# One fused attention and feed-forward kernel: the pair of quads combined from the pv bank, jobs and extras placed anew

## The reference

```
q  = layernorm(x) @ Wq.T + bq, scaled by 1/4       16 heads of 16 columns
k  = ctx @ Wk.T + bk        v = ctx @ Wv.T + bv
a  = softmax(q k^T) v        for each head          512 x 512 scores
y  = x + a @ Wo.T + bo
h  = (layernorm(y) @ W1[b].T + b1[b]) @ W2[b].T + b2[b]
out = y + h
```

## Time and profile before

| | us |
|---|---|
| median of 3 runs | 575.1 |
| profiled execution | 571.25 |
| its span | 569.5 |
| TensorE busy (PE) | 529.5, 93% |
| DVE busy | 442.7, 78% |
| ACT busy | 383.8, 67% |
| GpSimd busy (POOL) | 277.4, 49% |

### The profile page before, as it was taken

The page is one execution under the profiler, slowest core; times in us unless marked ns, Lnnn a source line. Parts: engine busy times, 40 slices in busy tenths (PEclk is TensorE's granted clock), DMA queues, the critical chain, the costliest instruction groups (busy, mean ns, idle before and its releaser), DMA issues.

```text
span 569.5 us, 13271 instructions
## 1 busy us (share of the span) xinstructions
PE 529.5 (93%) x4229; PEld 334.3 (59%) x4229; DVE 442.7 (78%) x805; ACT 383.8 (67%) x707; POOL 277.4 (49%) x314
## 2 busy tenths in 40 slices
PE   8899999999999889997999979999799989899997
PEld 6564556665666565664666656566466656354556
DVE  4888886898788986899778997789968887776114
ACT  6347778777876658775676747767487777667732
POOL 3946434576247814566335743367234782107211
PEclk9989999999999989999999989999899999898999
DMA  6773064615355243523446133470425424340201
GB/s 205 203 242 95 3 150 114 231 33 135 101 156 174 59 131 76 224 74 75 111 113 232 28 94 93 114 258 2 120 70 141 157 59 131 79 168 0 88 9 37
DMA packets 34367, 65.29 MB, mean 115 GB/s; under 512 B 9810, under 2 KB 11930, under 8 KB 32282
## 3 DMA queue, kind: packets, MB, share of 16 engines
q1 hardware_dynamic: 34330, 64.81, 38.7%
HBM read 34.65 MB, written 4.44 MB: 69 GB/s over the span
## 4 chain that ended last, share of the span: by engine, by line
PE 67%; DVE 12%; POOL 9%; issue 6%; ACT 2%; DMA 1%; SPq 0%; DVEq 0%; POOLq 0%; ACTq 0%
PE pv L560 16%; PE st L546 13%; PE misc L673 9%; PE nat L529 8%; PE misc L645 7%; DVE neg_max L1037 7%; PE misc L632 7%; POOL b_part L1334 3%; POOL b_part L1329 3%; POOL y L1322 2%; DVE y L1103 2%; ACT probs L861 2%; DVE stats L1048 2%; PE misc L609 1%; PE nat L585 1%
## 5 line engine op out<-in xcount | busy, mean ns | idle before, releaser
L1037 DVE TENSOR_REDUCE neg_max<-nat 128x1 f32<-128x512 f32 x512 | 328.4, 679 | 64.1 <-PE nat L529 62.2
L861 ACT ACTIVATE probs<-st 128x512 f32<-128x512 f32 x505 | 289.9, 598 | 123.7 <-PE st L546 111.5
L529 PE MATMUL nat<-ks,qs 63*128 63x512 f32 x512 | 241.3, 495 | 13.0 <-DVE neg_max L1037 10.4
L546 PE MATMUL st<-qs,ks 64*128 64x512 f32 x505 | 233.2, 489 | 4.6 <-ACT probs L861 3.9
L546 PEld LDWEIGHTS st<-qs,ks 64*128 64x128 f32 x505 | 92.1, 189 | 78.6 <-ACT probs L861 54.4
L560 PE MATMUL pv<-probs,vs 128*32 128x512 f32 x1024 | 126.0, 610 | 0.0
L529 PEld LDWEIGHTS nat<-ks,qs 63*128 63x128 f32 x512 | 94.2, 188 | 29.4 <-DVE neg_max L1037 22.6
L673 PE MATMUL misc<-w_in 64*128 64x256 f32 x512 | 75.6, 387 | 0.0
L1305 POOL TENSOR_TENSOR attnT<-pair_ctx,inv_sum 128x512 f32<-128x512 f32 x15 | 19.3, 1285 | 113.1 <-DMA inv_sum<-inv_dram 113.1
L560 PEld LDWEIGHTS pv<-probs,vs 128*32 128x32 f32 x1024 | 27.0, 110 | 55.8 <-issue 44.4
L673 PEld LDWEIGHTS misc<-w_in 64*128 64x128 f32 x512 | 54.4, 195 | 6.3 <-issue 0.8
(11 more groups left out here) (152 smaller groups left out, 695.7 us busy)
## 6 DMA issues: line engine op xcount, KB each, us to landing
ks<-hi SPq DMA_DIRECT2D x64, 128.0 KB, 2.6
qs<-hi SPq DMA_DIRECT2D x64, 128.0 KB, 2.5
w_in<-w SPq DMA_DIRECT2D x8, 1024.0 KB
w_in<-w2T SPq DMA_DIRECT2D x8, 1024.0 KB
ctx_in<-ctxT SPq DMA_DIRECT2D x8, 512.0 KB, 3.8
ks<-lo SPq DMA_DIRECT2D x32, 128.0 KB, 2.6
qs<-lo SPq DMA_DIRECT2D x32, 128.0 KB, 2.5
y<-x SPq DMA_DIRECT2D x8, 512.0 KB, 3.5
```

Source lines behind the costliest of these rows:

```text
L529: mm(ring(at)[:, :], qs[rows, 2 * g + jj, c * P:(c + 1) * P], ks[rows, 2 * g + jj, :], start=True, stop=True).then_inc(nat_done, 1)
L546: mm(st_of(u, prep)[:, :], ks[rows, 2 * g + jj, kc * P:(kc + 1) * P], qs[rows, 2 * g + jj, :], start=True, stop=True).then_inc(st_done, 1)
L861: act.activation(probs[kc % 4][:, j, :], st_of(u, prep)[:, :], ACT.Exp).then_inc(exp_done, 1)
L1037: dve.tensor_reduce(neg_max[:, g % 2, col:col + 1], ring(at_nat(n))[:, :], AX.X, ALU.max, negate=True).then_inc(max_done, 1)
```

## The change

The combine on DVE reads the odd quad from `pv_bank` and no longer from ACT's copy `odd_sum`. The copy stays, since the sums are gathered from it, and the combine still waits for it. The next pair's first pv block waits for the combine (`odd_out`) and no longer for the copy.

The units of the jobs Q, WO, V, YT, Z and W21 and of the extras on ACT and DVE are other ones: the even quad's mask, the odd copy of the first pair (35 to 38), the combine of the second pair (9 to 3), the inversion of the first pair's sums (59 to 52), the split of ctx (40 to 42), the statistics of x (33 and 35 to 50) and its normalisation (57 and 61 to 58). The lists of SP and GpSimd are in another order: on SP load_ctx ahead of the stack of quad 3, load_x, `store_max(b, 2)` and `save_inverse(b, 0)` earlier, the stores of the output and load_y later; on GpSimd the split of k ahead of `divide(b - 1, 1)`, `ctx_rest` and `add_bo` behind `inverse_root` and three `v_stack`.

In the lead of turn 0 the first group's maxima are transposed and copied ahead of natural score 17 (before: ahead of 18), and score 17 takes the next slot of the ring.

`nat`, `row_max` and `store_max` take an optional slot number for this. The diff, cut to its core:

```diff
--- before.py
+++ after.py
@@ -68,23 +68,23 @@
-Q_AT = (12, 12, 12, 13, 13, 13, 15, 15, 15, 16, 16, 17)
-WO_AT = (19, 20, 21, 21, 22, 23, 24, 24)
-V_AT = (28, 28, 29, 29, 30, 31, 32, 32)
-YT_AT = (34, 34)
-Z_AT = (36, 36, 36, 37, 38, 39, 40, 41)
-W21_AT = (44, 45, 47, 48, 52, 52, 53, 55, 55, 57, 57, 59, 60, 61, 61, 62, 62, 62)
+Q_AT = (12, 12, 12, 12, 13, 13, 14, 15, 15, 16, 16, 16)
+WO_AT = (20, 20, 20, 21, 22, 23, 24, 24)
+V_AT = (27, 28, 28, 29, 30, 31, 32, 32)
+YT_AT = (34, 35)
+Z_AT = (37, 38, 38, 38, 40, 40, 40, 41)
+W21_AT = (44, 45, 46, 47, 48, 48, 52, 52, 54, 55, 56, 56, 57, 59, 60, 60, 61, 62)
 
 EVEN_AT = (24, 50)
-MASK_AT = (29, 58)
-ODD_AT = (35, 2)
-PAIR_AT = (39, 9)
-INVERT_AT = (59, 7)
+MASK_AT = (36, 54)
+ODD_AT = (38, 2)
+PAIR_AT = (39, 3)
+INVERT_AT = (52, 7)
 Y_NORM_AT = (32, 32)
-CTX_AT = 40
-X_STATS_AT = (33, 35)
+CTX_AT = 42
+X_STATS_AT = (50, 50)
 X_AGGREGATE_AT = 50
-X_NORM_AT = (57, 61)
+X_NORM_AT = (58, 58)
@@ sync turn @@
-                if post:
-                    stack_quad(b, 3)
                 if load:
                     wait_apart(sp, ctx_ready, b + 1)
                     load_ctx(b + 2)
                 if post:
+                    stack_quad(b, 3)
                     gather_sums(b - 1, 1)
+                if load:
+                    wait_apart(sp, norm_ready[0], 4 * (b + 2))
+                    load_x(b + 2)
+                if post:
                     save_inverse(b - 1, 1)
                 store_max(b, 1)
                 if post:
                     spread_inverse(b - 1, 1)
-                if load:
-                    wait_apart(sp, norm_ready[0], 4 * (b + 2))
-                    load_x(b + 2)
-                if post:
                     wait_apart(sp, w21_done, 2 * b)
                     wait_apart(sp, b2_part_ready, b)
                     load_ffn(b)
+                store_max(b, 2)
                 if prep:
                     stack_quad(b + 1, 0)
-                store_max(b, 2)
                 gather_sums(b, 0)
                 store_max(b, 3, prep)
                 if prep:
                     stack_quad(b + 1, 1)
+                    stack_quad(b + 1, 2)
+                save_inverse(b, 0)
                 if post:
                     store_out(b - 1, 0)
                     store_out(b - 1, 1)
-                if prep:
-                    stack_quad(b + 1, 2)
                 load_y(b)
                 if prep:
                     store_max(b + 1, 0)
-                save_inverse(b, 0)
                 spread_inverse(b, 0)
@@ tensor: pv @@
-                        wait(pe, odd_copied, pair)
+                        wait(pe, odd_out, pair)
@@ tensor: the lead of turn 0 @@
             for n in range(FIRST_LEAD):
-                if n == 16 + TURN_AFTER:
-                    maxT(0, 0, slice(0, P)).then_inc(maxT_done, 1)
-                nat(0, n)
+                if n == 17:
+                    pe.wait_ge(max_done, 17)
+                    nc.tensor.transpose(ring(18)[:, 0:P], neg_max[:, 0, :], ident[:, :]).then_inc(maxT_done, 1)
+                nat(0, n, 19 if n == 17 else None)
@@ vector: odd_quad @@
-                dve.scalar_tensor_tensor(pair_ctx[:, :], odd_sum[:, :], half_hi[:, 0:1], even_ctx[:, :],
+                dve.scalar_tensor_tensor(pair_ctx[:, :], pv_bank[:, :], half_hi[:, 0:1], even_ctx[:, :],
                                          ALU.mult, ALU.add).then_inc(odd_out, 1)
@@ vector: the lead of turn 0 @@
-                if n == 16 + TURN_AFTER:
-                    max_row(0, 0)
+                if n == 17:
+                    dve.wait_ge(maxT_done, 1)
+                    dve.tensor_copy(max_hi[:, :], ring(18)[0:16, 0:P]).then_inc(max_done, 1)
...
-                row_max(0, n)
+                row_max(0, n, 19 if n == 17 else None)
@@ gpsimd turn @@
                     xT_split(b + 1)
                 if post:
                     v_stack(b, 3)
+                if prep:
+                    qk_split(b + 1, 1)
+                if post:
                     divide(b - 1, 1)
                 if prep:
-                    qk_split(b + 1, 1)
                     qk_split(b + 1, 0)
                 if post:
                     inverse_root(1, b - 1)
...
                 if post:
                     add_b2(b - 1)
                 if load:
-                    ctx_rest(b + 2)
                     inverse_root(0, b + 2)
-                add_bo(b)
                 if prep:
                     v_stack(b + 1, 0)
                     v_stack(b + 1, 1)
+                    v_stack(b + 1, 2)
+                if load:
+                    ctx_rest(b + 2)
+                add_bo(b)
                 divide(b, 0)
-                if prep:
-                    v_stack(b + 1, 2)
```

More of the change, by code:

```diff
@@ L364, in stack_quad, with store_max @@
                                      src[rows, which, g // 2, :].bitcast(F32)).then_inc(stacked[g], 16)
-            def store_max(b, g, prep=True):
-                wait_apart(sp, max_done, RING * (b + g // 3) + at_maxT(g, prep) + 1)
+            def store_max(b, g, prep=True, at=None):
+                wait_apart(sp, max_done, RING * (b + g // 3) + (at_maxT(g, prep) if at is None else at) + 1)
                 wait_apart(sp, st_done, UNITS * (b - 1) + 16 * g + 16)
@@ L495, in _ @@
             load_ctx(1)
-            store_max(0, 0)
+            store_max(0, 0, True, 18)
             stack_quad(0, 3)
@@ L519, in keep_warm, with nat @@
                     mm(misc[2 + t][:, :], hi[rows, 1, 0, 0:P], hi[rows, 0, 0, :], start=True, stop=True)
-            def nat(b, n):
+            def nat(b, n, at=None):
                 g, c, (jj, jp) = n // 16, n % 16 // 4, NAT_HEADS[n % 4]
@@ L525, in nat @@
                     wait(pe, stacked[g], STACKS * (b + 1))
-                at = at_nat(n)
+                at = at_nat(n) if at is None else at
                 wait(pe, max_done, RING * b + {0: -1, 1: 0, 2: -2}.get(at, at - 2))
@@ L1029, in _, with row_max @@
         def _(dve):
-            def row_max(b, n):
+            def row_max(b, n, at=None):
                 g = n // 16
@@ L1036, in row_max @@
                 col = 8 * jp + 4 * jj + n % 16 // 4
-                dve.tensor_reduce(neg_max[:, g % 2, col:col + 1], ring(at_nat(n))[:, :], AX.X, ALU.max,
+                dve.tensor_reduce(neg_max[:, g % 2, col:col + 1], ring(at_nat(n) if at is None else at)[:, :], AX.X, ALU.max,
                                   negate=True).then_inc(max_done, 1)
```

## The result

The changed kernel takes 549.6 us (median of 4 runs, 547.8 to 551.5) against 575.1 us in the same session: ratio 0.956, 95% interval 0.951 to 0.961. I had forecast 555, with a range from 549.5 to 563, so the time lies 0.1 us inside the fast end. The profiled execution took 547.8 us with a span of 545.9 and a mean granted clock of 0.994; that of before had 571.25, 569.5 and 0.979.

What follows compares the result with a forecast made beforehand. Bound: loop turns stop for a DVE combine with two SBUF inputs waiting for GpSimd, then TensorE's clock drops. 19.6 + 0.7 + 4.1 - 4.2 = 20.2, say 20 us, off the 575.1 median: 555 us, range 549.5 to 563.

Steps and rivals of the forecast that it cites:

- (c): SP's chain is late and DVE waits at u = 3, by 1.5 us in six turns: 564 us; chance 0.1.
- (d): New places pay more: nothing lost at WO and Z, 2 us more at W21's end: 549 us; chance 0.08.
- What bounds the kernel: At u = 42, turns 2 to 5: two-SBUF-input combine waits 4.87 us for GpSimd, TensorE stops, low clock can cost 1.7 us.
- Part 1, the stretch of u = 42: Combine reads the pv bank: pv block u = 42 to 50 takes 6.9 us against 11.84, 19.6 us in four turns.
- a wait under 0.6 us: Sign of being right: W21's wait for DVE's output half stays under 0.6 us.
- rival (b): Chain of b2 on GpSimd replaces the stop before W21: 2.5 us a turn gained, not 4.9, 565 us; chance 0.12.
- rival (a): GpSimd still stops a combine with one SBUF input, at u = 39 and u = 3: 594 us; chance 0.03.
- Part 1, the other side: Next pv block waits for DVE's combine, not ACT's copy: half a microsecond of cover at u = 42, cost 0.
- Part 2, u = 3: Second pair's combine moves from u = 9 to 3, behind `divide(b, 0)`'s product: cover 1.6 us, cost 0.
- Part 3, W21: Two W21 pieces fewer at the turn's end: 0.9 us saved in the last turn, 0.45 in seven others, 4.1 together.
- Part 3, WO and Z: Uneven pieces around u = 19 and 39 leave TensorE waiting: 0.3 us each in seven turns, 4.2 us lost.
- Part 4: Statistics of x at u = 50, reordered GpSimd and SP lists, and turn 0's lead: about 0 us.

Runs made afterwards that it cites:

- the bank alone: The kernel before with only the combine's source changed to the pv bank and the next pair's block waiting for the combine: 564.9 us, ratio 0.983.
- the separate measurement: A small kernel of its own: GpSimd runs 1, 2 or 4 adds, DVE the combine from SBUF or PSUM; the combine took 1.5 us or 0.74 us.

## Why the prediction was right, step by step

*The number.* The time lies 5.4 us from the forecast and 0.1 us inside the fast end of the range. Single executions of the changed kernel reach from 547.8 to 554.2 us, so that the median fell inside is luck. Most of the 5.4 us is one term that was not there, the 4.2 us of WO and Z. The range did not fit its text either: it was said to take in (c), which stood at 564, and most of (d), which stood at 549, and both lie outside of 549.5 to 563.

*What bounds the kernel.* Right for the combine and the ring: taking away the last part of GpSimd's run (`ctx_rest`, 2.35 us) shortened the combine by 2.3 us. The low clock is tied to them less firmly than I had it. Before, TensorE paused twice (1.93 and 1.49 us) and the low level followed in four loop turns of four; with one pause of 1.5 us it followed in two of four where `ctx_rest` moved, and in none of four where the combine read the copy. None of the loop turns of after has it; its low stretches lie in the lead and in the last turn, in another execution of it also in turn 0.

*Part 1, the stretch of u = 42.* The mechanism held and 6.9 us was exact for the bank alone (6.93). In the full change it is 7.32, 18.1 us in the four turns and not 19.6. My layout on turn 3's old times let output half 0 start at 264.0, when the adds end. Those times moved: V's earlier place brings TensorE to the pv block sooner, 1.7 us behind the start of the adds instead of 2.0, and output half 0 waits 0.98 us for them. W21 waits 0.74 us, so one sign that I had named, a wait under 0.6 us, did not come. That is rival (b) in small: 0.4 us of the 2.5 a turn that it named, and no low clock with it. Turns 1 and 6: forecast 7.15, measured 7.18 and 7.19. The Trainium skill (SBUF - State Buffer, "Who interferes with whom") says that a VectorE instruction with at most one SBUF input does not contend with GpSimd; the trace agrees, 0.74 us in all 15, and rival (a) is gone. It also says that the second one waits until the first instruction finishes, by which I had put the change at 3 us; the runs show both, 1.5 us in the separate measurement and 4.87, 3.36 and 2.58 in three versions of this kernel. The kernel's own rows decided the sum, and that was right, though only two of the three rows that I called on ran beside GpSimd (rows 10 did not).

*Part 1, the other side.* Half right. At u = 39 the block does not wait for DVE, as said. For the second pair I named no price, since u = 3 lies seven units ahead of the block; left at u = 9 it costs 1.5 us a turn, and moved to u = 6 it gave 7.3 us between the medians. The bank read and the move are one edit in two places.

*Part 2, u = 3.* The combine never waits for the product, as said. I gave 1.6 us of cover; `divide(b, 0)` ended at 281.23 and the combine started at 283.55, 2.3 us behind. GpSimd, then DVE:

```profile
279.95 1.28 POOL L1305 TENSOR_TENSOR attnT<-pair_ctx,inv_sum 128x512 f32<-128x512 f32 x1
```

```profile
283.55 0.74 DVE L1090 SCALAR_TENSOR_TENSOR pair_ctx<-pv,half_hi,even_ctx 128x512 f32<-128x512 f32 x1
```

The move was not quite free: the stretch from u = 2 to 10 ahead of turns 1 and 6 was 6.95 us and is 7.32, where the combine now stands ahead of the group's last maxima on DVE. With the start of turn 7 that is 1.0 us in all; its cause was not tested. Ahead of the other turns it cost nothing (7.54 to 7.57, before 7.53 to 7.57).

*Part 3, W21.* 4.1 forecast, 4.7 measured, but not made up as I had it. The units at the end of a turn gave 7.0 us, since also in the seven turns that are not the last u = 58 gave nearly its full 0.9 us and not half. u = 42 and 50 took 2.4 back. For that I had booked 0.4 a loop turn at u = 42 in part 1, where it was 0.07, and nothing at u = 50, where it was 0.33.

*Part 3, WO and Z.* This is the term that failed: 4.2 us lost, and measured nothing. Windows of before for u = 18, 26, 34, then 50 and 58:

```profile
237.88:245.84 7.96, 7.91 (x68) 5.56 (x67) 6.04 (x11) 5.31 (x11) 7.64 (x9) 1.00 0.81 306
245.84:253.78 7.94, 7.76 (x83) 5.06 (x81) 7.78 (x19) 5.55 (x11) 3.64 (x6) 1.00 0.19 43
253.78:263.15 9.37, 8.96 (x83) 6.25 (x82) 8.59 (x16) 7.37 (x14) 9.06 (x8) 1.00 0.03 6
274.99:282.64 7.65, 7.58 (x63) 4.89 (x62) 5.74 (x14) 5.14 (x11) 3.43 (x7) 1.00 0.59 156
282.64:291.52 8.88, 7.86 (x77) 5.14 (x76) 5.33 (x10) 7.74 (x18) 1.77 (x4) 1.00 0.09 31
```

and the same stretches of after:

```profile
232.30:240.25 7.95, 7.91 (x67) 5.49 (x66) 5.90 (x11) 5.18 (x11) 4.25 (x5) 1.00 0.44 172
240.25:247.89 7.64, 7.55 (x82) 5.20 (x80) 7.48 (x19) 5.06 (x10) 3.00 (x5) 1.00 0.46 103
247.89:257.22 9.33, 9.22 (x83) 6.12 (x82) 8.05 (x14) 7.69 (x15) 9.02 (x8) 1.00 0.01 2
264.54:272.52 7.98, 7.98 (x64) 4.83 (x62) 7.42 (x19) 6.05 (x11) 4.31 (x8) 1.00 0.51 131
272.52:280.52 8.00, 7.35 (x70) 4.50 (x69) 5.31 (x9) 7.21 (x18) 4.15 (x6) 1.00 0.66 207
```

In the stretch of WO (first rows) TensorE is busy 7.91 of 7.96 and 7.95 us, and the stretch has not grown; old places for both jobs gave 549.8 us. I had argued from the units, one with three pieces and one with none. That with the engine full over the whole stretch a wait inside a unit only opens where another closes is how I now read it; that is argued, not tested. Z's stretch (third rows, 9.37 and 9.33) was less full, 8.96 of 9.37 us, and has not grown in the loop turns either; in turns 1 and 6 it grew from 8.97 to 9.18, while V's stretch ahead of it fell from 7.61 to 7.41. The busy time of just these stretches, which I had not read, speaks against the term for WO. Without it the sum is 24.4 us, and 571.25 - 24.4 = 546.9 on the profiled execution against 547.8 measured; on the median 550.7 against 549.6. That closeness is partly luck as well: part 1 gave 1.5 us less than its 19.6, u = 2 to 10 cost 1.0, the lead's scatter 0.8, while V's stretch gave 1.8 where I had 0 (most of what part 1 lacks is the other side of it) and one low stretch less in the last turn 1.2. The last rows show what W21's places do: 0.33 more in u = 50, 0.88 less in u = 58.

*Part 4.* Statistics at u = 50: with W21's old places that stretch is 7.66, before 7.65, so 0. The lead: 0.

*The rivals.* (c) did not come. (d), 549 us, to which I gave 0.08, was the closest of all: nothing lost at WO and Z, and W21 worth 0.6 us more where it had 2.

*Medians and the clock.* In this kernel's executions time follows the mean granted clock: after, 547.8 us at 0.994, 549.0 at 0.991, 550.2 at 0.988, 551.3 to 552.1 at 0.984 and 554.2 at 0.981. Before lay at 0.964 to 0.979. At like clock (0.979 and 0.981) the two are 571.5 and 554.2, 17.3 us apart. So, as an estimate from few executions, about 8 of the 25.5 us go with the clock. I had taken a gain read from one profiled execution, one of before's fastest (571.25), off its median (575.1); between the profiled executions the gain is 23.5 us, between the medians 25.5.

## What to carry to other kernels

When one instruction takes several times its usual time, look at what the other engines run over exactly that interval and at what ends with it: here exchanging two lines of the other engine's list gave 13.6 of 25.5 us, and a PSUM source took the wait away. When a reader of a PSUM bank becomes another engine, the time at which that engine gets to it becomes the bank's release (here 1.5 us a turn later at u = 9), so the edit has to be placed anew at every site. Before pricing a rearranged list of matmuls piece by piece, read the busy time of TensorE in that stretch alone: where it was full here, at 7.91 of 7.96 us, another order changed nothing.

## What the runs showed of the hardware that was not expected

- A DVE instruction with two SBUF inputs (128x512, 0.74 us alone) waited through the rest of four GpSimd adds in the loop turns of this kernel (3.36 and 2.58 us in two versions, and 4.87 us where an instruction of 2.35 us stood behind the adds), but for one running add in a kernel of its own (1.5 us behind 1.26 us adds, for k = 1, 2 and 4). What decides between the two was not settled.
- Both sides pay: GpSimd's instruction behind a DVE one that got in took 1.59 instead of 1.29 us in the kernel, and 1.71 instead of 1.26 in the separate measurement.
- The same instruction with one input in PSUM took 0.74 us in 15 of 15 cases, 13 of them beside a GpSimd instruction, and in all 18 trials of the separate measurement.
- One fall to 1.2 GHz costs 1.0 to 1.2 us in a stretch with a pause of TensorE, and 1.6 in one without (8.43 against 6.80). The time of one kernel follows the mean clock: 547.8 to 554.2 us over 0.994 to 0.981. In the two kept profiles of it the falls and the lead make up the whole difference.
- A stop in one stretch does not always bring the low level: with `ctx_rest` moved, the same pause of 1.5 us was followed by it in two loop turns out of four, and in none of four where the combine read the copy.
